# Feed-forward stage of a mixture of experts: when TensorE reads the numbers of its experts, and two of its waits

## The chip, the cores and the metric

The kernel runs on one core of a Trainium2 chip. The metric is the time of one execution on the device in microseconds, as the median of several runs.
## The reference, cut to what matters

Two layers follow one another on 256 x 64 = 16384 tokens of 128 features. The first is a convolution-like layer with two products over pairs, gates and norms; it takes the first half of the time and is not touched by the change. The second is a feed-forward layer with 8 experts, of which each token takes the two with the highest probability:

```python
logits = xt @ Wr + br
probs = jax.nn.softmax(logits, axis=-1)
top_p, top_idx = jax.lax.top_k(probs, TOP_K)                 # TOP_K = 2
weights = top_p / top_p.sum(axis=-1, keepdims=True)
xn = (xt - mu) * jax.lax.rsqrt(var + LN_EPS)
xe = xn[None, :, :] * ln_g[:, None, :] + ln_b[:, None, :]
h = gelu(jnp.einsum('end,edh->enh', xe, W1) + b1[:, None, :])  # 128 -> 512
y = jnp.einsum('enh,ehd->end', h, W2) + b2[:, None, :]         # 512 -> 128
out = (weights[:, :, None] * sel).sum(axis=1)                  # sel: y of the two chosen experts
```

The result is added to the tokens.

## The kernel before, in words

**Tiles.** The tokens are sorted by expert into two lists, one for the first choice of each token and one for the second. Each list is cut into 70 tiles of 256 rows (`CUT = 70`, `TILES = 140`), and all rows of a tile belong to one expert. The rows of list 1 come from `row_dram`. Its results, with the token's running sum and its normalized row, are scattered to `row2_dram`, from where list 2 reads them; the results of list 2 are scattered to `out`. The weights of all experts lie in SBUF as pairs of f16 numbers (a high part and a rest), and so do the activations: each product is done as three matmuls, high by high, rest by high, high by rest.

**Steps.** Every engine runs the same helper, `two_lists` (L105): for each list some single steps, then a hardware loop whose body holds six steps (`RING = 6`), then single steps again. Each engine gives a list of stages with a lag: at step n the stage of lag k works on tile n - k. For TensorE the order in a step is: transposes of tile n-1 (`xT`, L1175), the first half of the up products of tile n-2 (`up` with q=0, L1195), the second half (q=1), the down products of tile n-3 (`down`, L1211). ScalarE copies the transposed rows (L684) and does the gelus (L691, L694). VectorE normalizes the rows of a new tile in list 1 (L1016), takes the rests (L1021, L1026) and adds the result into the rows (L1032). GpSimd scatters the finished tile in two halves (L528). SyncE loads the rows of a tile (L411) into one of six places, after it has waited for the scatter of the tile that had the place before (L404).

**Experts.** Which expert a tile has is known only at run time. A table in SBUF (`experts`) has two integers for each step: the expert of the tile in its down products and that of the tile in its up products. At the head of each step `load_experts` (L1188) reads both into registers of TensorE's sequencer, with one TENSOR_LOAD. From them the addresses of the weights are computed: one FUSED_REGOPS instruction of the sequencer for each new address, at L1206 and L1208 (8 in a step), L1217 (1), L1225 and L1228 (8).

**Waits of TensorE.** `xT` waits for the rows (`xn_done` in list 1, `r_loaded` in list 2) and for `xT_lo` of two tiles before, since it writes into the PSUM bank that VectorE's L1021 then read (L1181). Each half of `up` waits for `xT_lo` of its own tile and for `h_full` of two tiles before, since it writes into the bank that ScalarE's L694 then read (L1201). `down` waits for `y_done` of the tile before (L1216) and for `h_parts` of its own tile (L1220). [...]

Of the kernel before, what the change touches and what calls it, by code (L numbers as in the profile page):

```python
# [17 lines left out]
NE, D, H = 8, 128, 512  # L18
# [83 lines left out]
                stage(n - lag)  # L102

def two_lists(eng, stages, depth, before=None):  # L105

    longest = max(lag for lag, _ in stages)
    for second, low, high in ((0, 0, CUT), (1, CUT, TILES)):

        def step(n, u):  # L110
            if before:
                before(n)
            for lag, stage in stages:
                if not isinstance(n, int) or low <= n - lag < high:
                    stage(n - lag, (u - lag) % RING, second)

        def single(n0, n1):
            for n in range(n0, n1):
                step(n, n % RING)

        first, last = -(-(low + longest + depth) // RING), high // RING
        single(low, first * RING)
        with eng.Fori(first, last) as t:
            for u in range(RING):
                step(t * RING + u, u)
        single(last * RING, high + longest)
# [11 lines left out]
def build(nc, x, pp, cp, z_mask, ln_w, ln_b, lnc_w, lnc_b, gate_w, gate_b, lin_w, lin_b, eg_w, eg_b,  # L138
          as_w, as_b, Wr, br, ffn_g, ffn_b, W1, b1, W2, b2, out, g_dram, row_dram, row2_dram):
    with ExitStack() as ctx:  # L140
# [3 lines left out]
        def sem(name):  # L144
            return ctx.enter_context(nc.semaphore(name))
# [86 lines left out]
        experts = work[0:1, 1408:1408 + 2 * EROWS].bitcast(i32).rearrange("p (n v) -> p n v", v=2)  # L232
# [59 lines left out]
        s = type("S", (), S)  # L292
# [8 lines left out]
        h_psum, h_full, h_parts = ([sem(f"{name}{q}") for q in range(2)] for name in ("h_psum", "h_full", "h_parts"))  # L301
# [12 lines left out]
        def _(sp):  # L314
# [69 lines left out]
            for table, blank, g0 in ((row_dram, pad, 0), (row2_dram, pad2, NE)):  # L384
                for q in range(0, NE, 4):
                    _, counts = nc.values_load_multi_w_load_instructions(nti[0:1, 1, g0 + q:g0 + q + 4], [mybir.EngineType.SP],
                                                                         min_val=0, max_val=N)
                    for k in range(4):
                        sp.dma_start(pair(table[bass.ds(counts[k] + (q + k) * CAP, TR), :]), blank).then_inc(s.pads_out, 16)
# [11 lines left out]
            def load_tile(n, u, second):  # L401
# [9 lines left out]
                sp.dma_start(Rw[:, u, :, 0:width], table[bass.ds(first * TR, TR), :].rearrange("(p b) r -> p b r", b=HALVES)).then_inc(r_loaded[u], 16)  # L411

            two_lists(sp, [(0, load_tile)], RING)

        @block.gpsimd
        def _(pool):
# [105 lines left out]
            def store_tile(n, u, second):  # L522

                for b in range(HALVES):
# [6 lines left out]
                                            bounds_check=last_token if second else last_row, oob_is_err=False).then_inc(o_stored[u], 16)  # L531

            two_lists(pool, [(3, store_tile)], 1)
            for u in range(RING):
                pool.wait_ge(o_stored[u], 16 * HALVES * len(range(u, TILES, RING)))

        @block.scalar
        def _(act):
# [58 lines left out]
            for h in range(IC):  # L597
# [44 lines left out]
                def weights(b):  # L642

                    _, j0, j1 = BATCHES[b]
                    act.wait_ge(s.tail, TAIL * b + 15)
                    for col, scale in ((WLO, 1.0), (WHI, -1.0)):
                        a = act.activation(rows[:, j0:j1, col:col + 1].rearrange("p j o -> p (j o)"), choices[b].m12[:, DL, :],
                                           ACT.Sigmoid, scale=scale)
                    a.then_inc(s.w_given, 1)  # L650
# [35 lines left out]
            def gelus(n, u, q):  # L686
# [7 lines left out]
                act.activation(Hf[:, q, :], ps[HB[hs]][:, :], ACT.Gelu, scale=1.0 / SCALE).then_inc(h_full[q], 1)  # L694

            two_lists(act, [(1, xT_high), (2, lambda n, u, second: gelus(n, u, 0)), (2, lambda n, u, second: gelus(n, u, 1))], 2)

        @block.vector
# [340 lines left out]
        def _(pe):  # L1039
# [135 lines left out]
            def xT(n, u, second):  # L1175
                if second:
                    pe.wait_ge(r_loaded[u], (n // RING) * 16 + 16)
                else:
                    pe.wait_ge(s.xn_done, n + 1)
                if not isinstance(n, int) or n >= 2:  # L1180
                    pe.wait_ge(s.xT_lo, n - 1)  # L1181
                for b in range(HALVES):
                    i = pe.transpose(ps[u % 2][:, b * P:(b + 1) * P], Rw[:, u, b, ROW:ROW2], ident[:, :])  # L1183
                i.then_inc(s.xT_psum, 1)

            chosen = []

            def load_experts(n):  # L1188

                _, chosen[:] = nc.values_load_multi_w_load_instructions(  # L1190
                    experts[:, bass.ds(n, 1), :].rearrange("p n v -> p (n v)"), [mybir.EngineType.PE],
                    min_val=0, max_val=NE - 1,
                    skip_runtime_bounds_check_because="each is an expert of the table, or the zero beside them")

            def up(n, u, q):  # L1195

                hs = 2 * (u % 2) + q
                x_ = chosen[1]
                pe.wait_ge(s.xT_lo, n + 1)
                if not isinstance(n, int) or n >= 2:  # L1200
                    pe.wait_ge(h_full[q], n - 1)  # L1201
                for k in range(2):
                    c = (2 * q + k) * P
                    w = lambda r: W1h[:, bass.ds(x_, 1), r, c:c + P].rearrange("p a m -> p (a m)")
                    o = ps[HB[hs]][:, k * TR:(k + 1) * TR]
                    pe.matmul(o, w(0), xTp[:, u % 2, 0, :], start=True, stop=False)  # L1206
                    pe.matmul(o, w(0), xTp[:, u % 2, 1, :], start=False, stop=False)  # L1207
                    i = pe.matmul(o, w(1), xTp[:, u % 2, 0, :], start=False, stop=True)  # L1208
                i.then_inc(h_psum[q], 1)

            def down(n, u):  # L1211

                x_ = chosen[0]
                for b in range(HALVES):
                    if not isinstance(n, int) or n >= 1:
                        pe.wait_ge(y_done[b], n)  # L1216
                    pe.matmul(ps[4 + b][:, 0:D], allone[:, :], b23[:, bass.ds(x_ * D, D)], start=True, stop=False)  # L1217
                for k in range(HC):
                    if k % 2 == 0:
                        pe.wait_ge(h_parts[k // 2], n + 1)  # L1220
                    hs = 2 * (u % 2) + k // 2
                    w = lambda r: W2h[:, bass.ds(x_, 1), r, k, :].rearrange("p a d -> p (a d)")
                    hk = lambda r, b: Hp[:, hs, r, k % 2 * TR + b * P:k % 2 * TR + (b + 1) * P]
                    for b in range(HALVES):
                        pe.matmul(ps[4 + b][:, 0:D], hk(0, b), w(0), start=False, stop=False)  # L1225
                        pe.matmul(ps[4 + b][:, 0:D], hk(1, b), w(0), start=False, stop=False)  # L1226
                    for b in range(HALVES):
                        i = pe.matmul(ps[4 + b][:, 0:D], hk(0, b), w(1), start=False, stop=(k == HC - 1))  # L1228
                        if k == HC - 1:
                            i.then_inc(y_psum[b], 1)  # L1230

            two_lists(pe, [(1, xT), (2, lambda n, u, second: up(n, u, 0)), (2, lambda n, u, second: up(n, u, 1)),
                           (3, lambda n, u, second: down(n, u))], 2, before=load_experts)

# [21 lines left out]
```

## Time and profile before

| | |
|---|---|
| median of 3 runs | 1040.82 us (1039.2 to 1045.29) |
| profiled execution | 1043.44 us, its span 1041.4 us |
| busy in the span: TensorE, weight loads, VectorE, ScalarE, GpSimd | 791.3, 665.7, 631.6, 583.3, 560.8 us |
| feed-forward steps | 140, from about 526 us of the span to its end |
| granted clock of TensorE, mean over the span | 0.862 |

The span is the time from the first to the last instruction; the profiled execution's own time lies 2 us above it. Matmuls overlap in the array: a matmul's recorded duration is longer than the distance to the next one, so the pace is read from the distances of the starts.
### The profile page before, as it was taken

Reading aid. Unit: us, or ns where it says so; the run is one execution under the profiler, and the core shown is the slowest. Engines: PE = TensorE matmul, PEld = TensorE weight load, DVE = VectorE, ACT = ScalarE, POOL = GpSimd, SP = SyncE. Lnnn points to the kernel's source line nnn. Section 1 sums busy time; section 2 is a strip of 40 time slices with the busy share of each in tenths; the row PEclk is TensorE's granted clock in tenths of the full one; section 3 lists DMA queues with packets and bytes.
Section 4 is the critical chain, followed back from the end, with each engine's and each line's share of the span. In section 5 each row is a group of like instructions: output and inputs, shape, how many; then the busy total and the mean of one; then the engine's idle time right before and its main releaser. Section 6 shows DMA issues by size and latency. Waiting matters only on the chain. (4 is left out here: it accounts for less than half of the span.)

```text
span 1041.4 us, 25571 instructions
## 1 busy us (share of the span) xinstructions
PE 791.3 (76%) x7318; PEld 665.7 (64%) x7319; DVE 631.6 (61%) x2144; ACT 583.3 (56%) x1167; POOL 560.8 (54%) x581
## 2 busy tenths in 40 slices
PE   0667798687778377629278999999968899899995
PEld 0455688466668266512067877888757788787874
DVE  3555511877450588863257777878745666666663
ACT  1467752788332355231056766777646667676763
POOL 0756600443127788677725555656554555555554
PEclk9999999566579567555579999999998999999998
DMA  9497511566102244715123333333323333434441
GB/s 238 104 271 243 162 53 44 185 179 199 41 14 78 95 126 135 233 46 193 51 79 117 120 103 121 115 116 112 109 66 108 109 112 111 113 109 116 115 116 35
DMA packets 123849, 124.78 MB, mean 120 GB/s; under 512 B 22233, under 2 KB 91120, under 8 KB 123796
## 3 DMA queue, kind: packets, MB, share of 16 engines
q1 hardware_dynamic: 89476, 80.65, 27.3%
q0 software_dynamic: 15296, 34.64, 9.5%
q10 hardware_dynamic: 19024, 8.86, 3.0%
q8 instruction: 25, 0.41, 0.2%
q14 instruction: 28, 0.22, 0.1%
HBM read 77.40 MB, written 49.09 MB: 121 GB/s over the span
## 5 line engine op out<-in xcount | busy, mean ns | idle before, releaser
L1026 DVE TENSOR_TENSOR AB<-AB 128x512 f16<-128x512 f32 x280 | 192.1, 686 | 73.0 <-ACT AB L694 68.7
L528 POOL DMA_INDIRECT row_dram<-B x140 | 143.7, 1027 | 112.6 <-DVE B L1032 77.0
L528 POOL DMA_INDIRECT out<-B x140 | 139.6, 997 | 117.5 <-DVE B L1032 92.1
L691 ACT ACTIVATE AB<-ps 128x512 f16<-128x512 f32 x280 | 168.2, 601 | 41.2 <-PE ps L1208 40.6
L1225 PE MATMUL ps<-PPb,AB 128*128 x1120 | 185.3, 219 | 0.0
L1226 PE MATMUL ps<-PPb,AB 128*128 x1120 | 185.1, 219 | 0.0
L694 ACT ACTIVATE AB<-ps 128x512 f32<-128x512 f32 x280 | 169.2, 604 | 0.0
L1206 PE MATMUL ps<-B,PPb 128*128 128x256 f16 x560 | 154.5, 276 | 0.5 <-issue 0.5
L1207 PE MATMUL ps<-B,PPb 128*128 128x256 f16 x560 | 154.0, 275 | 0.0
L1208 PE MATMUL ps<-B,PPb 128*128 128x256 f16 x560 | 154.0, 275 | 0.0
L1228 PE MATMUL ps<-PPb,AB 128*128 x1120 | 153.9, 219 | 0.0
L467 POOL TENSOR_TENSOR rs<-vv,half 128x12 f32<-128x12 f32 (+2 forms) x40 | 76.1, 1903 | 106.2 <-DVE vv L905 50.4
L684 ACT ACTIVATE B<-ps 128x256 f16<-128x256 f32 x140 | 53.8, 384 | 140.7 <-PE ps L1183 140.7
L1183 PE MATMUL ps<-ident,B 128*128 128x128 f32 x280 | 59.4, 295 | 74.6 <-issue 32.1
L1032 DVE SCALAR_TENSOR_TENSOR B<-ps,B 128x128 f32<-128x128 f32 x280 | 97.0, 347 | 27.3 <-PE ps L1228 26.3
L1226 PEld LDWEIGHTS ps<-PPb,AB 128*128 128x128 f16 x1120 | 109.6, 98 | 0.0
L1225 PEld LDWEIGHTS ps<-PPb,AB 128*128 128x128 f16 x1120 | 109.4, 98 | 0.1
L1183 PEld LDWEIGHTS ps<-ident,B 128*128 128x128 f32 x280 | 29.0, 144 | 96.9 <-issue 79.7
L1228 PEld LDWEIGHTS ps<-PPb,AB 128*128 128x128 f16 x1120 | 86.0, 98 | 0.0
L488 POOL DMA_INDIRECT row_dram<-rows,idx x64 | 65.7, 1027 | 25.8 <-issue 18.7
L477 POOL DMA_INDIRECT row_dram<-rows,idx x64 | 62.6, 979 | 30.8 <-issue 17.3
L1016 DVE TENSOR_SCALAR B<-B 128x128 f32<-128x128 f32 x140 | 43.5, 364 | 57.2 <-DMA B<-row_dram 56.6
(218 smaller groups left out, 1620.9 us busy)
## 6 DMA issues: line engine op xcount, KB each, us to landing
B<-row_dram SPq DMA_DIRECT2D x70, 264.0 KB
B<-row_dram SPq DMA_DIRECT2D x70, 136.0 KB
rows<-in_x SPq DMA_DIRECT2D x32, 256.0 KB, 5.3
rows<-in_L_conv_protein_pair SPq DMA_DIRECT2D x16, 512.0 KB, 4.9
g_dram<-work ACTq DMA_DIRECT2D x32, 256.0 KB, 3.3
work<-g_dram SPq DMA_DIRECT2D x32, 256.0 KB, 2.8
ABT<-in_x SPq DMA_DIRECT2D x32, 256.0 KB, 3.0
ABT<-in_L_conv_protein_pair SPq DMA_DIRECT2D x16, 512.0 KB, 4.8
```

The lines of the kernel that those rows point to most:

```text
L528: pool.indirect_dma_start(out_rows if second else row2_dram, bass.IndirectOffsetOnAxis(ap=Rw[:, u, b, at:at + 1].bitcast(u32), axis=0), Rw ...
L691: act.activation(Hp[:, hs, 0, :], ps[HB[hs]][:, :], ACT.Gelu, scale=1.0 / SCALE)
L694: act.activation(Hf[:, q, :], ps[HB[hs]][:, :], ACT.Gelu, scale=1.0 / SCALE).then_inc(h_full[q], 1)
L1026: dve.tensor_tensor(Hp[:, hs, 1, :], Hf[:, q, :], Hp[:, hs, 0, :], ALU.subtract).then_inc(h_parts[q], 1)
L1032: dve.scalar_tensor_tensor(Rw[:, u, b, 0:D], ps[4 + b][:, 0:D], Rw[:, u, b, w:w + 1], Rw[:, u, b, 0:D], ALU.mult, ALU.add).then_inc(y_done ...
L1183: i = pe.transpose(ps[u % 2][:, b * P:(b + 1) * P], Rw[:, u, b, ROW:ROW2], ident[:, :])
L1206: pe.matmul(o, w(0), xTp[:, u % 2, 0, :], start=True, stop=False)
L1207: pe.matmul(o, w(0), xTp[:, u % 2, 1, :], start=False, stop=False)
L1208: i = pe.matmul(o, w(1), xTp[:, u % 2, 0, :], start=False, stop=True)
L1225: pe.matmul(ps[4 + b][:, 0:D], hk(0, b), w(0), start=False, stop=False)
L1226: pe.matmul(ps[4 + b][:, 0:D], hk(1, b), w(0), start=False, stop=False)
L1228: i = pe.matmul(ps[4 + b][:, 0:D], hk(0, b), w(1), start=False, stop=(k == HC - 1))
```

## The change

TensorE's registers for the experts become two pairs, used in turn by even and odd steps. The pair of step n+1 is loaded in step n, between the two halves of the up products, and no longer at the head of step n+1; only the first step of a list loads its own. At the head of each step `begin` takes a copy of each of the two registers (`nc.snap`), which the step then uses. Two waits are left out: that for `xT_lo` in `xT`, and that for `h_full` in both halves of `up`. Both are implied by waits that TensorE has passed in the step before: that for `xT_lo` by the wait of `up` for the same tile, that for `h_full` by the wait of `down` for `h_parts`, which VectorE gives only after it has read what `h_full` tells of. `two_lists` gets an argument `always` for the stage that loads: it runs at every step but the last. The other engines' programs are unchanged.

```diff
-def two_lists(eng, stages, depth, before=None):
+def two_lists(eng, stages, depth, before=None, always=None):
...
             if before:
-                before(n)
+                before(n, u, low)
             for lag, stage in stages:
-                if not isinstance(n, int) or low <= n - lag < high:
+                if not isinstance(n, int) or low <= n - lag < high or stage is always and n + 1 < high + longest:
                     stage(n - lag, (u - lag) % RING, second)
...
                 else:
                     pe.wait_ge(s.xn_done, n + 1)
-                if not isinstance(n, int) or n >= 2:
-                    pe.wait_ge(s.xT_lo, n - 1)
...
+            PEQ = [mybir.EngineType.PE]
+            pairs = [[pe.alloc_register(f"expert{v}_{w}") for w in range(2)] for v in range(2)]
             chosen = []
 
-            def load_experts(n):
-
-                _, chosen[:] = nc.values_load_multi_w_load_instructions(
-                    experts[:, bass.ds(n, 1), :].rearrange("p n v -> p (n v)"), [mybir.EngineType.PE],
-                    min_val=0, max_val=NE - 1,
-                    skip_runtime_bounds_check_because="each is an expert of the table, or the zero beside them")
+            def load_experts(n, v):
+                pe.reg_load(pairs[v], experts[:, bass.ds(n, 1), :].rearrange("p n v -> p (n v)"))
+
+            def begin(n, u, low):
+                if isinstance(n, int) and n == low:
+                    load_experts(n, u % 2)
+                chosen[:] = [nc.snap(r, PEQ, min_val=0, max_val=NE - 1) for r in pairs[u % 2]]
 
             def up(n, u, q):
 
                 hs = 2 * (u % 2) + q
                 x_ = chosen[1]
                 pe.wait_ge(s.xT_lo, n + 1)
-                if not isinstance(n, int) or n >= 2:
-                    pe.wait_ge(h_full[q], n - 1)
...
-            two_lists(pe, [(1, xT), (2, lambda n, u, second: up(n, u, 0)), (2, lambda n, u, second: up(n, u, 1)),
-                           (3, lambda n, u, second: down(n, u))], 2, before=load_experts)
+            def next_experts(n, u, second):
+                load_experts(n + 1, (u + 1) % 2)
+
+            two_lists(pe, [(1, xT), (2, lambda n, u, second: up(n, u, 0)), (0, next_experts), (2, lambda n, u, second: up(n, u, 1)),
+                           (3, lambda n, u, second: down(n, u))], 2, before=begin, always=next_experts)
```

## Rows read from the trace of the kernel before

**Rows 1.** Busy time by stretch: middle of list 1, late list 2; PEclk is the granted clock.

```profile
600.00:700.00 100.00, 91.99 (x1141) 79.88 (x1141) 77.74 (x199) 69.78 (x144) 58.69 (x57) 1.00 0.36 114
...
900.00:1000.00 100.00, 90.94 (x1147) 80.17 (x1145) 64.53 (x144) 70.15 (x144) 55.89 (x58) 1.00 0.40 113
```

**Rows 2.** Timeline of TensorE's array, one step of list 2: start, duration, idle before.

```profile
902.55 0.28 PE L1228 MATMUL ps<-PPb,AB 128*128 x2
903.08 0.41 PE L1183 MATMUL ps<-ident,B 128*128 128x128 f32 x2 [0.25 <-issue]
...
904.66 0.27 PE L1217 MATMUL ps<-AB,allone 128*128 x2
...
906.00 0.27 PE L1228 MATMUL ps<-PPb,AB 128*128 x2
```

**Rows 3.** TensorE's sequencer by line, 902.2 to 905.66: count, duration ns, first to last start.

```profile
L1190 PEldq TENSOR_LOAD <-work x1: 539/539/539, 902.2 to 902.2; - x1
L1190 PEldq FUSED_REGOPS  x1: 74/74/74, 905.5 to 905.5; - x1
L1177 PEldq FUSED_REGOPS  x1: 80/80/80, 902.8 to 902.8; - x1
L1181 PEldq EVENT_SEMAPHORE  x1: 51/51/51, 903.0 to 903.0; - x1
L1201 PEldq EVENT_SEMAPHORE  x2: 51/51/51, 903.1 to 903.7; - x2
L1206 PEldq FUSED_REGOPS  x4: 46/46/46, 903.2 to 904.1; - x4
L1208 PEldq FUSED_REGOPS  x4: 46/46/46, 903.4 to 904.2; - x4
L1217 PEldq FUSED_REGOPS  x1: 60/60/60, 904.3 to 904.3; - x1
L1225 PEldq FUSED_REGOPS  x4: 46/48/60, 904.5 to 905.3; - x4
L1228 PEldq FUSED_REGOPS  x4: 46/46/51, 904.6 to 905.4; - x4
```

**Rows 4.** Timeline of VectorE in the same step: the second add of the finished tile.

```profile
903.68 0.35 DVE L1032 SCALAR_TENSOR_TENSOR B<-ps,B 128x128 f32<-128x128 f32 x1
```

**Rows 5.** The loads of the experts, list 1 (first row) and list 2, as rows 3.

```profile
L1190 PEldq TENSOR_LOAD <-work x65: 532/548/838, 536.6 to 759.9; - x65
...
L1190 PEldq TENSOR_LOAD <-work x58: 532/537/606, 807.3 to 1007.2; - x58
```

**Rows 6.** Timeline of list 1: one of the six places, from one tile to the next.

```profile
650.23 0.41 PE L1183 MATMUL ps<-ident,B 128*128 128x128 f32 x2
...
659.81 0.28 PE L1228 MATMUL ps<-PPb,AB 128*128 x2
...
662.86 1.31 POOL L528 DMA_INDIRECT row_dram<-B  x1 [0.30 <-issue]
...
667.03 0.55 SPq L411 DMA_DIRECT2D B<-row_dram  x1
...
669.47 0.60 DVE L1016 TENSOR_SCALAR B<-B 128x128 f32<-128x128 f32 x2 [1.21 <-DMA B<-row_dram]
...
670.78 0.41 PE L1183 MATMUL ps<-ident,B 128*128 128x128 f32 x2 [0.18 <-issue]
```

**Rows 7.** Timeline of list 2: issue of a tile's load and the tile's transposes.

```profile
881.51 0.33 SPq L411 DMA_DIRECT2D B<-row_dram  x1
...
885.54 0.30 PE L1183 MATMUL ps<-ident,B 128*128 128x128 f32 x1 [0.28 <-issue]
```

**Rows 8.** Timeline of list 1 where rows came late: VectorE, then TensorE's down products.

```profile
610.30 0.60 DVE L1016 TENSOR_SCALAR B<-B 128x128 f32<-128x128 f32 x2 [1.92 <-DMA B<-row_dram]
...
612.69 0.55 PE L1217 MATMUL ps<-AB,allone 128*128 x2
```

**Rows 9.** SyncE's own register loads, one register each, in list 2.

```profile
L410 SPq TENSOR_LOAD <-work x58: 275/282/415, 800.4 to 998.5; - x58
```

## The prediction

> **What bounds the kernel now.** I read the stretches first, then TensorE's timeline in one step, then its sequencer, then the round of a tile through memory.
>
> The feed-forward stage fills the second half of the span. [...] From the first transpose at 903.08 to the bias matmuls at 904.66 and the last down matmuls at 906.00 everything follows without a hole: 1.58 + 1.34 + 0.11 for the last two = 3.03 us of array work in a step. But between the last down matmuls (902.55, 0.11 for two, so 902.66) and the transposes (903.08) the array stands still for 0.42, and the bracket says "issue" [rows 2]. A step takes 223.3 / 64 = 3.49 us in list 1 and 199.9 / 57 = 3.51 in list 2 [rows 5].
>
> Who fills the hole is seen in the sequencer. In that step it does 23 instructions [rows 3]. Their durations add up: load 0.539, its address 0.074, L1177 0.080, three EVENT_SEMAPHOREs 0.153, eight address instructions of the up products 0.368, L1217 0.060, four at L1225 0.203, four at L1228 0.189 = 1.67. The step lasts from the load at 902.2 to 0.13 after the next load's address at 905.5, 3.43; so 1.76 / 23 = 0.077 lies behind each instruction, and the starts come in an even beat (eight at L1206 and L1208 between 903.2 and 904.2) without a longer hole. So the sequencer never waits; it is the bound, and the array only follows. At the load's start, 902.2, the array has 0.43 of work in hand; load, L1177 and L1181 take 0.8.
>
> [...]
>
> **The change part by part.**
>
> *The waits.* They are satisfied long before and carry no time of waiting; what goes is the instruction. Three EVENT_SEMAPHOREs go in a step, L1181 and twice L1201. By duration and gap each is 0.051 + 0.077 = 0.128; by the distance of their starts (903.0, 903.1, 903.2) nearer 0.11 [rows 3]. I take 0.115: -0.35 us a step (-0.32 to -0.38). In one step of six another register instruction carried one of them; I leave that out.
>
> *The load* keeps its address instruction and its 0.54 [rows 3, 5]. Moved between the halves of up it costs the sequencer the same. With a sequencer that is the bound the place is worth 0: the hole is smaller and lies elsewhere. If it were not the bound, up to the hole of 0.42 would go. No DMA or other queue is moved past, and what stands behind the load now is the second half of up and the down products: they come 0.1 to 0.3 later behind the transposes.
>
> [...]
>
> *Sum for the sequencer:* list 2: -0.35 + 0.02 = -0.33, a step of 3.51 - 0.33 = 3.18. List 1: -0.35 + 0.12 = -0.23, 3.26. Both stay above the array's 3.03.
>
> *What is late next.* (a) The adds: VectorE's second add ends at 904.03, 1.37 after the array's last down matmul; the next down products need it and take 1.45: 2.8 in a round, under 3.18 [rows 2, 4]. (b) The round of a tile's place. In list 1: transposes 650.23, down products end 659.92, second scatter issued 662.86, next load issued 667.03, its rows normalized from 669.47 to 670.07, transposes 670.78 [rows 6]. Six steps take 20.55 (3.43 each, a quiet stretch), and the rows are ready only 0.71 early. Of the round only two steps and the way to the down products run at TensorE's pace; from 659.92 to 670.07 are 10.15 us of adds, scatters and DMA that stay. With TensorE faster: 20.55 - 0.66 of slack - 2 x 0.23 + 0.2 (down products later behind transposes) = 19.6, or 3.27; taking a little off for the second tight place of the six, 3.29. That is -0.14 a step and not -0.23. Stalls that list 1 has already (rows late at 610.30 hold VectorE, which holds the adds, so that the two bias matmuls at 612.69 stand 0.3 apart [rows 8]) have less slack in front of them; I leave their 0.06 a step as they are. So list 1 goes from 3.49 to 3.35. In list 2 a load issued at 881.51 is used at 885.54; at 2.44 from issue to use in list 1 [rows 6, 7] it is 1.6 early. Six steps shorter by 2.0, two of them ahead of the down products (0.66) give the place 1.3 less: still early, with 0.3 left. I take 1 us off the whole list for that.
>
> *Total.* List 1: about 66 of 70 steps x 0.14 = 9 us. List 2: about 64 x 0.33 = 21, less 1 = 20. The first and last steps of each list wait for single tiles and stay. 29 us in all: the profiled execution goes from 1043.4 to 1014, its span from 1041.4 to 1012. That execution was 2.6 above the median, so the median goes from 1040.8 to **1012**.
>
> **The rivals.**
>
> *1. The round does not bind list 1.* For it: over most of rows 6's kind the slack is over 1 us, and only some places are tight. Then 66 x 0.23 = 15 and 21: 36 us, 1005. Chance 0.15.
>
> *2. The round binds harder.* The queue of scatters and loads gets 10% more traffic in a time; if scatter and load grow with it, list 1 keeps its 3.49 and list 2 gives half: 10 us, 1031. Against it: the DMA engines' share is 0.36 to 0.40 [rows 1]. Chance 0.10.
>
> *3. The change does not do what it says for the time.* [...] Against it stands the even beat of the sequencer in rows 3. Chance 0.05. [...]
>
> [...]
> **How the numbers follow.** Forecast 0.64; faster by over 0.5% (5 us, about what a measurement of this kernel can tell from no change) holds it and rivals 1 and 2: 0.89. Same 0.05, slower 0.06. The range reaches down to rival 1 with the waits at 0.128 (36 + 3, 1001) and up to a round that takes all of list 1 and some of list 2 (14 us left, 1027); rivals 3 and 4 and the far half of 2 stay outside, under 0.2.
>
> **What will show it.** In the profile after: no EVENT_SEMAPHORE at the lines of the two waits; one TENSOR_LOAD a step, still 0.54, between the halves of up; distance of two loads 3.18 in list 2, 3.35 in list 1; hardly any idle time before the transposes, and instead 0.1 or so before the second half of up; in list 1 more of TensorE's or VectorE's idle time ended by the rows' DMA. The prediction is wrong if list 2 stays above 3.35 with the three waits gone (the sequencer was not the bound), or if list 1 gains as much as list 2 does (the round has no hold), or if two loads stand in a step.

## The result

| | before | after |
|---|---|---|
| median of 8 runs each, same chip | 1041.61 us (1039.2 to 1045.5) | 1034.59 us (1031.14 to 1039.89) |
| ratio to before, 95% interval | | 0.993 [0.9901, 0.996] |
| profiled execution, its span | 1043.44, 1041.4 us | 1039.89, 1037.8 us |
| busy: TensorE, VectorE, ScalarE, GpSimd | 791.3, 631.6, 583.3, 560.8 us | 793.8, 627.6, 588.3, 568.3 us |

The change gains 7 us. The forecast was 29 (1012) and the range ended at 1027, so it was wrong. The sign is right and the size is off by a factor of four. The profiled execution of after is the slowest of its eight: the two spans differ by 3.6 us, the medians by 7, so the trace shows about half of the gain.

### The profile page after: what moved, and what is told of

Same layout as the page of the kernel before. It is cut to its first block and busy times, and to the rows that moved or that the text cites. A ratio compares the mean times of both kernels' runs of the same rounds, so it can differ in the third digit from the quotient of the medians.

```text
span 1037.8 us, 25289 instructions
## 1 busy us (share of the span) xinstructions
PE 793.8 (76%) x7318; PEld 657.8 (63%) x7319; DVE 627.6 (60%) x2144; ACT 588.3 (57%) x1167; POOL 568.3 (55%) x581
## 5 line engine op out<-in xcount | busy, mean ns | idle before, releaser
L528 POOL DMA_INDIRECT out<-B x140 | 148.7, 1062 | 98.4 <-DVE B L1032 55.9
L1206 PE MATMUL ps<-B,PPb 128*128 128x256 f16 x560 | 154.6, 276 | 0.0
L1205 PEld LDWEIGHTS ps<-B,PPb 128*128 x560 | 54.8, 98 | 69.9 <-issue 62.8
L1181 PE MATMUL ps<-ident,B 128*128 128x128 f32 x280 | 57.8, 289 | 41.4 <-DVE B L1016 29.9
```

The source lines that it names most:

```text
L528: pool.indirect_dma_start(out_rows if second else row2_dram, bass.IndirectOffsetOnAxis(ap=Rw[:, u, b, at:at + 1].bitcast(u32), axis=0), Rw ...
```

## The profile after

*List 2, the sequencer's part.* First the stretches (columns as in [rows 1]):

```profile
600.00:700.00 100.00, 91.32 (x1142) 78.10 (x1141) 77.35 (x202) 71.60 (x144) 58.54 (x57) 1.00 0.35 112
900.00:1000.00 100.00, 96.07 (x1201) 82.46 (x1199) 67.12 (x151) 74.28 (x150) 63.59 (x61) 1.00 0.39 119
```

In the same 100 us TensorE does 1201 matmuls in list 2 and did 1147 before [rows 1]. In list 1 it does 1142, and did 1141. What the steps gained lies in list 2. One step there, array and then sequencer by line:

```profile
902.55 0.28 PE L1227 MATMUL ps<-PPb,AB 128*128 x2
902.66 0.39 PE L1181 MATMUL ps<-ident,B 128*128 128x128 f32 x2
...
903.44 0.27 PE L1207 MATMUL ps<-B,PPb 128*128 128x256 f16 x1
903.72 0.28 PE L1205 MATMUL ps<-B,PPb 128*128 128x256 f16 x1
...
904.38 0.28 PE L1216 MATMUL ps<-AB,allone 128*128 x2
...
905.73 0.28 PE L1227 MATMUL ps<-PPb,AB 128*128 x2
905.84 0.39 PE L1181 MATMUL ps<-ident,B 128*128 128x128 f32 x2
```

```profile
L1194 PEldq FUSED_REGOPS  x1: 93/93/93, 902.2 to 902.2; - x1
L1189 PEldq FUSED_REGOPS  x1: 74/74/74, 902.9 to 902.9; - x1
L1189 PEldq TENSOR_LOAD <-work x1: 536/536/536, 903.0 to 903.0; - x1
L1205 PEldq FUSED_REGOPS  x4: 46/46/46, 902.4 to 903.9; - x4
L1207 PEldq FUSED_REGOPS  x4: 46/46/46, 902.5 to 904.0; - x4
L1216 PEldq FUSED_REGOPS  x1: 60/60/60, 904.1 to 904.1; - x1
L1224 PEldq FUSED_REGOPS  x4: 46/48/60, 904.3 to 905.1; - x4
L1227 PEldq FUSED_REGOPS  x4: 46/46/51, 904.4 to 905.2; - x4
```

Against [rows 2, 3] the reader is to see four things. The three EVENT_SEMAPHOREs are gone: 20 instructions in a step, not 23. The two copies and the address of the transposes are one instruction at L1194, 93 ns where L1177 had 80. The hole of 0.42 ahead of the transposes is gone: 902.55 + 0.11 = 902.66. What is left of it stands between the halves of up, 903.44 + 0.11 to 903.72, so 0.17. The step lasts 905.84 - 902.66 = 3.18, the number forecast for list 2.

But that is a quiet step. From the starts of the transposes, the mean over list 2 (tiles 77 to 139) is 3.49 before and 3.37 after; over list 1 (tiles 3 to 69) it is 3.49 before and **3.54** after. Added up along the two profiled executions: list 1 +3.5 us, the way from list 1 to list 2 -2.2, list 2 -7.5, and +2.4 ahead of tile 3, of which 1.6 lie ahead of the first transposes, where nothing was changed. Since the execution of after is 5 us above its median, the traces show that list 1 gained nothing, and not that it lost.

*List 1, where nothing was gained.* Timelines of one late tile (start, duration, idle before):

```profile
633.99 1.33 POOL L528 DMA_INDIRECT row_dram<-B  x1 [0.30 <-issue]
...
637.62 0.54 SPq L411 DMA_DIRECT2D B<-row_dram  x1
...
640.61 0.64 DVE L1016 TENSOR_SCALAR B<-B 128x128 f32<-128x128 f32 x2 [1.63 <-DMA B<-row_dram]
...
640.59 0.27 PE L1227 MATMUL ps<-PPb,AB 128*128 x2
641.31 0.44 PE L1181 MATMUL ps<-ident,B 128*128 128x128 f32 x2 [0.45 <-DVE B L1016]
```

The second scatter out of the place is issued at 633.99, the next load into it at 637.62, its rows reach VectorE at 640.61, and the array, which had finished its down matmuls at 640.70, waits until 641.31. That is the round of [rows 6], and here the rows are not 0.71 early but 0.61 late. Over the middle of list 1 (540 to 760), by line: busy, mean ns, idle before and what ended it. The first row is the kernel before, the others are the kernel after:

```profile
L1016 DVE TENSOR_SCALAR B<-B 128x128 f32<-128x128 f32 x126 | 39.4, 367 | 37.5 <-DMA B<-row_dram 36.8
```

```profile
L1016 DVE TENSOR_SCALAR B<-B 128x128 f32<-128x128 f32 x124 | 39.0, 374 | 38.6 <-DMA B<-row_dram 38.2
...
L1181 PE MATMUL ps<-ident,B 128*128 128x128 f32 x124 | 25.0, 283 | 3.3 <-DVE B L1016 3.2
```

VectorE stands 38 us at the norm for rows that have not landed, 0.6 for each of the 62 tiles. That is no new time: the kernel before has 37 there. VectorE comes to the norm early in both, and before, this idle time held TensorE for next to nothing (0.01 us a step, below). What is new is that TensorE comes early as well, so that a late tile now holds it. How much, the distances of the sequencer's instructions tell (each less the usual one of its kind): 0.27 us a step of list 1 pass at the head of the step, L1194, for rows that are not there, and nearly nothing did before (0.01 at L1181). The prediction had priced the instructions of the waits at 0.35.

## The experiments

The theory when they began: the sequencer's terms are right, and the round of a place takes the gain. Rivals: the waits' instructions were never worth 0.35; or the load in its new place costs what the waits gave.

### The two parts apart

e1 is the kernel before without the two waits. e2 is the kernel after with the two waits put back. e3 is the kernel after with the load behind the down products.

```diff
# e1, in the kernel before
                     pe.wait_ge(s.xn_done, n + 1)
-                if not isinstance(n, int) or n >= 2:
-                    pe.wait_ge(s.xT_lo, n - 1)
...
                 pe.wait_ge(s.xT_lo, n + 1)
-                if not isinstance(n, int) or n >= 2:
-                    pe.wait_ge(h_full[q], n - 1)
# e2, in the kernel after: the same four lines back
# e3, in the kernel after
-            two_lists(pe, [(1, xT), (2, ... up(n, u, 0)), (0, next_experts), (2, ... up(n, u, 1)), (3, ... down(n, u))], ...
+            two_lists(pe, [(1, xT), (2, ... up(n, u, 0)), (2, ... up(n, u, 1)), (3, ... down(n, u)), (0, next_experts)], ...
```

Expected of e1:

> The kernel before with the two waits of TensorE left out and nothing else; the load of the experts stays at the head of the step, ahead of the wait for the rows. Theory (the place of the load): after the change the load stands behind the wait for the rows, on the round of a tile through memory; 0.4 to 0.6 us more of that round run at the sequencer's pace, and list 1 went from 3.49 to 3.54 us a step although an unhindered step takes 3.1 and not 3.4. With the load back ahead of the wait: list 1 about 3.30, list 2 about 3.22 us a step, total near 1012 us, ratio to before 0.97. Rival A (a faster TensorE lengthens the round by contention of scatters and loads, whatever the order): list 1 stays at 3.5, list 2 at 3.37, total near 1034. Rival B (the waits are worth nothing, the 7 us come from the moved load): total 1041, no change to before.

Expected of e2:

> The changed kernel with the two waits put back: only the move of the load and the copies remain. Theory: the sequencer is the bound and has the copies on top, and the load lies on the round: list 1 about 3.65, list 2 about 3.55 us a step, 10 to 15 us slower than before, near 1055. Rival A: as before in list 1 (3.49), list 2 3.5, within 3 us of before. Rival B: the 7 us gain of the change, 1034.

Expected of e3:

> The changed kernel with one stage moved: the load of the next step's experts comes after the down products, the last thing of the step, and so ahead of the next wait for the rows; register pairs and copies stay. Theory: like the kernel with the waits alone left out, plus the copies' 0.12 us in list 1 and 0.02 to 0.05 in list 2: list 1 3.33, list 2 3.24 us a step, total near 1016, clearly under the changed kernel. Rival A: no difference to the changed kernel, near 1034. If the copies or the pairs were what eats the gain, this one stays near 1034 while the waits alone reach 1012.

Measured: e1 1026.88, ratio 0.9855 [0.9825, 0.9885]. e2 1058.11, 1.0145 [1.0113, 1.0178]. e3 1036.56, 0.9928 [0.9903, 0.9953]. The kernel before was at 1043.31 with these.

The waits alone bring 16 us; the other part alone costs 15, as expected; together they would give 2, and 7 came. So the kernel before with the waits alone left out is faster than the whole change (0.9855 against 0.993, with intervals apart): with six places the load's move and the copies took back more than half of what the waits gave. e3 missed its forecast of about 1016: the load at the end of the step is as good as the load in the middle of it, so between these two places nothing is gained. e1 missed too, by 15 us, and its trace shows why:

```profile
603.18 0.60 DVE L1016 TENSOR_SCALAR B<-B 128x128 f32<-128x128 f32 x2 [1.32 <-DMA B<-row_dram]
...
605.49 0.34 DVE L1032 SCALAR_TENSOR_TENSOR B<-ps,B 128x128 f32<-128x128 f32 x1
605.66 0.46 PE L1213 MATMUL ps<-AB,allone 128*128 x2
606.10 0.23 PE L1221 MATMUL ps<-PPb,AB 128*128 x1
```

The rows came 1.32 late, VectorE took norm, rests and adds after them in its fixed order, and the bias matmuls at L1213 waited for the second add: from the first of them to the first down matmul are 0.44 us where 0.11 is usual, the pattern of [rows 8]. Where TensorE meets the lateness differs by the place of its load: at the bias matmuls in e1 (0.22 us a step, of which 0.07 are there with eight places too, e6 below) and in e3 (0.13), at the transposes in the kernel after (0.27). It meets it in all three.

### A shorter round

e4 is the kernel after, in which SyncE reads the first row of the tile ahead of its wait for the scatter instead of behind it, which takes some 0.6 us out of each round. e8 is the same edit in the kernel before.

```diff
+                first = sp.value_load(first_row[:, bass.ds(n, 1)], min_val=0, max_val=NE * CT)
                 if not isinstance(n, int) or n >= RING:
...
-                first = sp.value_load(first_row[:, bass.ds(n, 1)], min_val=0, max_val=NE * CT)
                 sp.dma_start(Rw[:, u, :, 0:width], ...
```

Expected of e4:

> The changed kernel, and SyncE reads the number of the tile's first row ahead of its wait for the scatter and not behind it: about 0.8 us (register load 0.28 to 0.42, address arithmetic 0.15, assertion) leave the round of each place in both lists, TensorE's program is the changed one. Theory: four steps of TensorE close the round, so list 1 gets up to 0.2 us a step shorter, 3.54 to about 3.30, list 2 3.37 to about 3.22: total 1034 less 18 and 9, near 1008. Rival A (contention, the queues are full): the load issued earlier lands as late; total within 5 us of 1034.

Expected of e8:

> The kernel before, with SyncE's read of the first row ahead of its wait. The same edit took 17 us from the changed kernel. Theory: here the round is not what holds it, so 0 to 4 us: 1037 to 1042. If the edit helps by itself, whatever the bound: near 1025.

Measured: e4 1017.98, 0.9756 [0.973, 0.9782]; e8 1038.8, 0.9957 [0.994, 0.9974]. The same edit is worth 17 us on the kernel after, 10 less than expected, and 4 on the kernel before, as expected. From the second scatter to the next load's issue 3.05 us pass in e4 and 3.64 in the kernel after (means of list 1). The step of list 1 falls from 3.54 to 3.35. So half a microsecond in the round, on SyncE, whose instructions take 35 of the 100 us from 600 to 700 in the kernel after, moves TensorE by a fifth of a microsecond in each step.

### Eight places

The rows get eight places instead of six, in a part of SBUF that is free in this stage. e5 is the kernel after with it, e7 the kernel before, e6 the kernel of e1.

```diff
-RING = 6
+RING = 8
...
-        Rw = Bf[:, 0:RING * HALVES * ROW2].rearrange("p (s b r) -> p s b r", s=RING, b=HALVES)
+        Rw = rowsf[:, 0:RING * HALVES * ROW2].rearrange("p (s b r) -> p s b r", s=RING, b=HALVES)
```

Expected of e5:

> The changed kernel with eight places for the rows of tiles instead of six (and so eight steps in the loop's body); they lie in SBUF that the stage before has left. The first-row read of SyncE is where it was. Theory now: the changed TensorE program takes about 3.1 to 3.2 us a step when nothing holds it, and both lists are held by the round of a place through scatter and load. With eight places the round may take two steps more, about 6 us, and holds nobody: list 1 about 3.17 (from 3.54 in the profile), list 2 about 3.17 (from 3.37), total near 1000 us, ratio to before 0.96. Rival A (scatters and loads get slower as TensorE gets faster; bandwidth or queues): no better than 1030. Rival C (the copies and the load's new place eat the gain in TensorE's own program): 1034, since nothing in that program changes.

Expected of e6:

> Only the two waits left out, load at the head, and eight places. Theory: the program without the copies has 0.05 to 0.1 us less in a step than the changed one; with the round out of the way the sequencer alone decides: 3.12 in both lists, total near 996. If instead the load's place decides once the round is gone (the array's hole ahead of the transposes comes back), this one is slower than the changed kernel with eight places, by up to 0.1 us a step or 13 us.

Expected of e7:

> The kernel before with eight places. Theory: it is bound by the sequencer at 3.43 plus the loop's branch, the round had 1.2 us of slack in list 1; only the few stalls of list 1 and a quarter of the branch cost go: 3.45 a step in both lists, total 1034 to 1038. If the round already held the kernel before, it gains as much as the changed one, 30 us and more.

Measured, with before at 1043.04: e5 1007.55, 0.966 [0.9632, 0.9688]; e6 1010.41, 0.9677 [0.9653, 0.9701]; e7 1037.26, 0.9929 [0.9902, 0.9956].

e7 came as expected. e5 missed its forecast of about 1000 by 7 us and e6 its forecast of about 996 by 14; e11 and the account of the prediction's terms below say why.

This is the decisive comparison. With the round out of the way the change is worth 1037.26 - 1007.55 = 30 us; with six places 7. Without the change the two more places are worth only 6 us. (The loop's body has eight steps with eight places, so its branch, a COMPARE_BRANCH of 0.21 us at L123 on TensorE's sequencer, comes once in eight steps and not once in six; that is so in e5, e6 and e7 alike. In list 2 of the kernel before, which a shorter or longer round does not move, e7 gains 0.02 a step by it.) In e5 the middle of list 1 reads:

```profile
L1016 DVE TENSOR_SCALAR rows<-rows 128x128 f32<-128x128 f32 x128 | 39.9, 353 | 0.0
```

```profile
600.00:700.00 100.00, 97.25 (x1245) 85.51 (x1246) 84.78 (x217) 76.53 (x156) 67.01 (x63) 1.00 0.39 123
```

No idle time is left ahead of the norm, where it was 38.6, and TensorE does 1245 matmuls in the stretch instead of 1142. DMA's share rises to 0.39 and GpSimd's busy time to 67 without harm, so at this share the traffic, which rival 2 had given as its reason, does not bind. The round is a little longer with it: from the second scatter to the next load's issue the mean of list 1 is 3.54 before, 3.64 after and 3.9 in e5. The steps: e7 3.40 and 3.47, e5 3.22 and 3.24 us (list 1, list 2).

### A longer round

SyncE reads the first row a second time behind its wait, and the second value is not used: 0.6 us more in each round (from the second scatter to the next load 3.54 before and 4.16 in e10). e9 is this in the kernel after, e10 in the kernel before.

```diff
                 first = sp.value_load(first_row[:, bass.ds(n, 1)], min_val=0, max_val=NE * CT)
+                again = sp.value_load(first_row[:, bass.ds(n, 1)], min_val=0, max_val=NE * CT)
```

Expected of e9:

> The changed kernel (six places), and SyncE reads the first row twice behind its wait: about 0.4 to 0.5 us (register load 0.28 to 0.42 and assertion) more in the round of each place. Theory: the round holds both lists and is closed by four steps of TensorE, so up to 0.11 us a step: 10 to 14 us slower than the changed kernel, near 1046. If the round only holds at times: 5 us or less.

Expected of e10:

> The kernel before with the same second read behind SyncE's wait. Theory: the round has slack here (1.2 us in list 1, 1.6 in list 2), so the same 0.45 us cost 0 to 4 us: 1043 to 1047. If the round held the kernel before just as much: 10 us and more.

Measured, with before at 1043.82: e9 1054.86, 1.0111 [1.0081, 1.0141]; e10 1058.87, 1.0159 [1.0129, 1.0189]. For the kernel after that is 20 us, where 10 to 14 had been expected. For the kernel before it is 15 where 0 to 4 had been expected: a clear miss of the theory as it then stood. List 2 of the kernel before did not move (3.49 to 3.50), list 1 went from 3.49 to 3.66. So list 1 was at the edge of the round already before the change. With e8 this says where the edge is: 0.6 us less in the round brings the kernel before 4 us, 0.6 more costs it 15.

### Without the copies

e11 is e5 with the loads in the middle of the step but into fresh registers, so that the copies are needed only once in the hardware loop, at its turn. e12 is e11 with SyncE's read ahead of its wait as in e4.

```diff
-                chosen[:] = [nc.snap(r, PEQ, min_val=0, max_val=NE - 1) for r in pairs[u % 2]]
+                    chosen[:] = load_experts(n)
+                elif u == 0:
+                    chosen[:] = [nc.snap(r, PEQ, min_val=0, max_val=NE - 1) for r in around]
+                else:
+                    chosen[:] = ahead
...
-                load_experts(n + 1, (u + 1) % 2)
+                if u == RING - 1:
+                    pe.reg_load(around, of_step(n + 1))
+                else:
+                    ahead[:] = load_experts(n + 1)
```

Expected of e11:

> The changed kernel with eight places, without the copies: each step's experts are read into registers of their own, at the same place between the halves of up, and only at the end of the loop's body a fixed pair is used and copied. In list 1 seven of eight steps lose one instruction of TensorE's sequencer (0.116 us from its start to the next one's), in list 2 two of five register operations (about 0.03). Theory (with the round out of the way the sequencer is the bound): list 1 3.22 to 3.12, list 2 3.24 to 3.21, together 7 to 9 us: near 999. If the array is the bound by now (3.03 of work in a step and small holes): 0 to 3 us.

Expected of e12:

> The one without copies, eight places, and in addition SyncE's read of the first row ahead of its wait. The same edit took 17 us from the changed kernel with six places. Theory: with eight places the round holds nobody, so within 3 us of the one without it, near 998. If some of the round is still on the path: 5 us and more.

Measured: e11 999.81, 0.9579 [0.9553, 0.9605]; e12 998.02, 0.9556 [0.953, 0.9583]. The steps of e11 are 3.09 and 3.23, against 3.22 and 3.24 with the copies: 0.13 a step in list 1 and 0.02 in list 2, which are the prediction's prices for the copies (0.12 and 0.02). In e11's list 1 the array has hardly a hole left:

```profile
600.00:700.00 100.00, 98.44 (x1300) 90.04 (x1300) 89.12 (x230) 79.99 (x163) 69.99 (x65) 1.00 0.42 130
```

e11 also tells what the load's place is worth once the round is out of the way, for it differs from e6 in that place and in one pair of copies for each eight steps. It is 10.6 us faster, with intervals apart. The steps are 3.09 and 3.23 against 3.23 and 3.26, and most of that is the length of the load itself: on the mean of list 1 it takes 0.55 us in e11 and 0.65 in e6, in list 2 0.55 and 0.57. That is where e6 missed: its load at the head was longer than the 0.54 it was priced at.

e12 shows the other side of e4: with eight places the 0.6 us of the round are worth no more than 2 us, which the measurement cannot tell from nothing, and not 17. Both are faster than all other kernels that were run.

### Does VectorE's order carry the lateness?

e13 is e10, and e14 is e1, each with the norm moved in VectorE's order from the head of the step to behind the first low part of h.

```diff
-            two_lists(dve, [(0, norm), (1, xT_low), (2, ... h_low(n, u, 0)), (3, ... mix(n, u, second, 0)), ...
+            two_lists(dve, [(1, xT_low), (2, ... h_low(n, u, 0)), (0, norm), (3, ... mix(n, u, second, 0)), ...
```

Expected of e13:

> The kernel before with SyncE's second read behind its wait, as in e10 (1058.87), and with VectorE's norm of a new tile moved in its fixed order from the head of the step to behind the first low part of h (it stays ahead of the adds of the step). Theory: e10 lost 15 us because rows that come late hold VectorE at the norm, in its fixed order, ahead of the low parts and of the adds that TensorE's next bias matmuls wait for; of e10's 0.159 us a step at those matmuls most goes, and the time falls to 1043 to 1050. Rival: what comes late is only the tile itself at its transposes; an order in which the norm comes later makes it later still, and the time stays at 1059 or rises.

Expected of e14:

> The kernel of e1 (both waits left out, the load at the head of the step; 1026.88) with the same move of the norm. Theory: TensorE's 0.216 us a step at the bias matmuls of list 1 falls by half or more, the price is a tile that is ready 0.2 to 0.3 us later for its transposes, and the sum is 1016 to 1023. Rival: the wait only changes its place, from the bias matmuls to the transposes, since the round of a place through memory is as long as before; 1025 to 1032.

Measured, with before at 1045.03: e13 1055.12, 1.0114 [1.0081, 1.0148]; e14 1038.64, 0.9945 [0.9923, 0.9967]. e13 lies a little below e10, with intervals that overlap, and above the 1043 to 1050 of its theory. e14 is about 10 us slower than e1, past both expectations. In both the wait at the bias matmuls is gone, and in e14 TensorE stands at the transposes instead (list 1 of e14, 540 to 760):

```profile
L1016 DVE TENSOR_SCALAR B<-B 128x128 f32<-128x128 f32 x124 | 37.1, 345 | 0.2 <-DMA B<-row_dram 0.2
...
L1181 PE MATMUL ps<-ident,B 128*128 128x128 f32 x125 | 27.4, 300 | 20.5 <-DVE B L1016 19.6 <-issue 0.9
```

But this is not the wait for late rows in another place. VectorE has 0.2 us of idle time at the norm: the rows have landed when it comes to it. The move has closed a new round, seen in the timelines of VectorE and TensorE in e14:

```profile
644.13 0.69 DVE L1026 TENSOR_TENSOR AB<-AB 128x512 f16<-128x512 f32 x1 [0.85 <-ACT AB L694]
644.74 0.60 DVE L1016 TENSOR_SCALAR B<-B 128x128 f32<-128x128 f32 x2
...
645.39 0.44 PE L1181 MATMUL ps<-ident,B 128*128 128x128 f32 x2 [0.31 <-DVE B L1016]
...
647.64 0.69 DVE L1026 TENSOR_TENSOR AB<-AB 128x512 f16<-128x512 f32 x1 [0.85 <-ACT AB L694]
```

The norm now stands behind the low part of h, which waits for the gelus; the transposes wait for the norm, the first half of up comes behind the transposes, and the next gelus wait for it. One turn takes 3.51 us (644.13 to 647.64), and the median step of list 1 is 3.51 in e14 and in e13 as well, though their waits and their rounds of a place differ. So the two runs tested another limit and say little on how lateness travels. How much of the kernel after's loss VectorE's order carries on, and how much is the round alone, stays open.

## Why the prediction was wrong

*The sequencer is the bound, and with a satisfied wait of these three goes the time of its EVENT_SEMAPHORE: right, the size a little too large.* With eight places the change brings 30 us. The prediction's terms without any round give 36 (its rival 1). In list 2 -0.33 a step was forecast (to 3.18), and e5 stands 0.23 below e7, at 3.24; in list 1 it was -0.23, and e5 stands 0.18 below. One reason is in the count: the prediction took three EVENT_SEMAPHOREs in every step and left out one in a turn of six. In list 2 of the kernel before (800 to 1010) the lines L1181 and L1201 have 49 and 109, so 158 in 59 steps, 2.7 a step; in one step of each turn an ALU_OP stands in the place of one at each line (10 of 36 ns at L1181, 10 of 32 ns at L1201). That is 0.03 a step at the price of 0.115. A quiet step of list 2 is at 3.18 or below (median 3.16 in e5), but once in a turn of the loop further instructions come on top (list 2 of e5: ALU_OPs of 36, 32 and 32 ns at L1177, L1215 and L1219, and at L123 one of 32 ns, the branch of 208 and a FUSED_REGOPS of 208), which the prediction counted for no step. How much of the rest they explain was not separated.

*The copies, 0.12 in list 1 and 0.02 in list 2: right* (e11 against e5: 0.13 and 0.02).

*The load keeps its 0.54, its place is worth 0: right for this change, and not in general.* In the kernel after the load's median stays at 0.54; its mean goes from 0.61 to 0.62 in list 1 and from 0.54 to 0.56 in list 2. e3 with the load last is as fast as the kernel after with it in the middle. But with the waits gone a load at the head is longer (median 0.67 in e6, 0.54 in e5, list 1). Against the copies of e5 the two nearly cancel; without copies, e11 against e6, the place in the middle is worth 10.6 us.

*"The round of a tile's place": the step that failed.* The prediction saw it and mis-sized it: by its sum the round takes 0.09 of 0.23 us a step in list 1 and 1 us in all of list 2. The runs say that it takes all of the gain of list 1, and in list 2 some 7 us (3.37 with six places, 3.24 with eight, 62 steps, less 1 us for the longer body of the loop). In time: the round costs 7 us by the prediction (36 less 29), and 23 by the runs (30 less 7). Where it went wrong:

- It took the slack from one quiet round (0.71 early, a step of 3.43), and left the stalls beside it as they were. Over list 1 of the kernel before, the way from the second scatter to the next load's issue is 3.4 us in the median, but one in ten takes over 4.0 and the longest 5.3; from the load's issue to the norm it is 2.6, 2.9 and 3.8. On the mean the rows are ready 1.2 us ahead of their transposes before, and still 0.8 in the kernel after, so it is not the mean that costs but the late ones. Every engine's program takes the tiles in order, so an early tile need not make up for a late one; that is an argument from the program, and no run took the late tiles away by themselves.
- It held these late ones to be a constant of 0.06 a step "as they are". With a faster sequencer each of them starts with less in hand. The steps of list 1 show it. Before: 3.42 in the median, 3.37 at the lower quarter, 3.69 at the upper tenth. After: 3.48, 3.15 and 3.94. The quick steps got quicker by 0.2, as forecast, and the slow ones slower by about the same.
- In list 2 it took 1.6 us of slack from one tile and 0.3 left. From a load's issue to its transposes the mean is 4.6 us before, 3.57 after and 4.07 in e4; the slack shrank by 1.0 on the mean, near the 1.3 that was worked out. Again the mean leaves slack and time is lost all the same: the step is 3.37 with six places, 3.28 with the shorter round (e4), 3.24 with eight places.

*Rival 2* had nearly the right result (1031) and a reason that explains little of it. It had 0.10. It wanted scatter and load to grow by a tenth; measured is 3.54 to 3.64 us from scatter to load's issue and 0.05 more from there to the norm, 0.15 in a round of six steps. That its number was close is luck. *Rival 4*, the load in two pieces, did not come: one TENSOR_LOAD in each step. What the kernel after would have been without its copies and with six places was not tried; the nearest is e1, without copies and with the load at the head.

*The signs named ahead.* Right: no EVENT_SEMAPHORE at the two waits, one load a step at 0.54 in the median, the small hole between the halves of up. Not seen: 3.18 and 3.35 between two loads on the mean (3.37 and 3.54), and idle time ended by the rows' DMA hardly rose (VectorE 36.8 to 38.2 us). "The prediction is wrong if list 2 stays above 3.35 with the three waits gone (the sequencer was not the bound)": it stayed at 3.37, and the conclusion in brackets would have been false; e5 against e7 was needed to see that a second limit had taken over at once.

## What to carry to other kernels

Before a faster engine is priced, list every ring that passes through it, and give each its slack as a distribution over the whole stage, not from one clean round; here 0.8 us of mean slack did not keep the gain. A cheap test of such a ring is to make it shorter by half a microsecond at an engine that is not the busiest, SyncE here: 4 us for the kernel before and 17 for the kernel after said which of them the ring binds. Making it longer told less here: it cost 15 and 20, since the ring of the kernel before was at its edge. Where a change shortens the sequencer's part of a step as this one does, widen the ring in the same change: 7 us with six places, 30 with eight.

## What the hardware showed that was not expected

TensorE's TENSOR_LOAD of two registers is not of one length. First row the kernel after in list 1, second the kernel of e1:

```profile
L1189 PEldq TENSOR_LOAD <-work x62: 533/543/860, 539.6 to 755.0; - x62
```

```profile
L1188 PEldq TENSOR_LOAD <-work x64: 533/670/804, 541.4 to 758.1; - x64
```

Its shortest is 0.53 to 0.54 everywhere; its median in list 1 is 0.54 to 0.57 in some kernels and 0.64 to 0.68 in others, in list 2 between 0.54 and 0.58. Place alone does not decide it: in e2 it stands in the middle of the step as in the kernel after, and its median in list 1 is 0.675. What lengthens it was not found.

The waits that were passed at once and stood as an EVENT_SEMAPHORE on TensorE's sequencer were not free. In the step of [rows 3] each takes 0.051 us and 0.055 to 0.084 pass behind it, and leaving out close to three in a step was worth 27 us of 1037 where the ring did not bind (e7 to e6), although the load grew by 0.06 us a step in list 1 and 0.03 in list 2 in the same move. The waits that stand on an instruction there for something else show no such price: at L1206, where the wait for the tile's own `xT_lo` is on the first address instruction of each half of up, all four take 46 ns [rows 3].
